# Holding back the last 16 sorted tiles for late tokens, with the last stage's lead-in beside them and the zero fills on SyncE's queue

## What is computed

```python
h = _L0_tok_ref(x, ...)                        # (64, 128, 256): rows of two tables
h = h + _L0_attn_ref(_layernorm(h), W_qkv, ...)     # linear attention, 16 heads
h = h + _L0_ffn_ref(_layernorm(h), sim_matrix, gates, q_proj, k_proj, v_proj, o_proj)

# in _L0_ffn_ref, E = 16 experts, HD = 128
rw = _gating(hidden_states, sim_matrix, gates)      # (b, t, E), two entries a token here
q = jnp.einsum('btc,ech,bte->bth', hidden_states, q_proj, rw)     # k and v alike
scores = jnp.where(causal[None], jnp.einsum('bqh,bkh->bqk', q, k) * scale, -jnp.inf)
ao = jnp.einsum('bqk,bkh->bqh', jax.nn.softmax(scores, axis=-1), v)
out = jnp.einsum('bth,ehc,bte->btc', ao, o_proj, rw)
```

## Time and profile before

| | |
|---|---|
| median of three executions | 995.45 us (992.7, 995.45, 995.6) |
| the profiled execution's own time | 992.72 us |
| its span, first to last instruction | 990.9 us |
| mean granted TensorE clock | 0.987 of full |
| busy in the span | PE 925.8, DVE 838.2, POOL 668.9, ACT 600.0 us |
| moved by DMA | 137.54 MB, mean 139 GB/s |

### The profile page before, as it was taken

How to read it: one execution, slowest core, us unless ns; L and a number is a source line. 1 busy time by engine, 2 the same in 40 slices (tenths; PEclk the granted TensorE clock), 3 DMA queues, 4 the chain that set the end, 5 groups by cost and what they waited for, 6 DMA issues and landing times.

```text
span 990.9 us, 20545 instructions
## 1 busy us (share of the span) xinstructions
PE 925.8 (93%) x5231; PEld 798.1 (81%) x5231; DVE 838.2 (85%) x2910; ACT 600.0 (61%) x1633; POOL 668.9 (68%) x881
## 2 busy tenths in 40 slices
PE   4999999999899989989999599999999999999998
PEld 4777788887777889979899578888888888888876
DVE  3789999999999987556665369999999999999998
ACT  4566676676667554435444266666666766666664
POOL 5447777777777655795000268888888888888885
PEclk9999999999999999989999889999999999999999
DMA  2113444444343349878898423333333333333231
GB/s 66 49 60 123 127 130 155 144 149 130 113 128 115 99 159 333 281 251 274 279 294 266 156 84 104 107 107 107 107 98 103 100 100 107 107 107 103 90 102 38
DMA packets 104762, 137.54 MB, mean 139 GB/s; under 512 B 13762, under 2 KB 91586, under 8 KB 104644
## 3 DMA queue, kind: packets, MB, share of 16 engines
q1 hardware_dynamic: 86196, 82.93, 26.6%
q0 software_dynamic: 18176, 52.45, 17.4%
q10 hardware_dynamic: 272, 0.79, 0.2%
HBM read 70.06 MB, written 66.06 MB: 137 GB/s over the span
## 4 chain that ended last, share of the span: by engine, by line
PE 60%; DVE 26%; issue 6%; POOL 3%; DMA 2%; ACT 2%; SPq 1%; POOLq 0%; DVEq 0%; ACTq 0%
PE bank L1655 16%; PE bank L1656 16%; PE bank L1657 16%; PE bank L1662 6%; DVE phi L1302 4%; DVE attn L1245 2%; DVE kvm L1321 2%; DVE stats L1258 2%; PE bank L1681 2%; DVE stats L1079 2%; DVE zden L1243 1%; PE bank L1899 1%; PE bank L1905 1%; POOL sorted_x L786 1%; DVE moments L1260 1%
## 5 line engine op out<-in xcount | busy, mean ns | idle before, releaser
L1655 PE MATMUL bank<-wo_hi,split_lo 128*128 128x512 f32 x512 | 214.6, 419 | 1.5 <-DVE split_lo L1623 0.8
L1656 PE MATMUL bank<-wo_lo,split_hi 128*128 128x512 f32 x512 | 203.3, 397 | 0.0
L1657 PE MATMUL bank<-wo_hi,split_hi 128*128 128x512 f32 x512 | 203.3, 397 | 0.0
L860 POOL DMA_INDIRECT row_y<-sorted_y,pair_now x128 | 130.7, 1021 | 31.2 <-issue 22.3
L1009 ACT ACTIVATE h<-bank,rwo 128x256 f32<-128x256 f32 x256 | 106.8, 471 | 26.5 <-PE bank L1657 13.9
L1657 PEld LDWEIGHTS bank<-wo_hi,split_hi 128*128 128x128 f32 x512 | 96.8, 189 | 23.1
L1655 PEld LDWEIGHTS bank<-wo_hi,split_lo 128*128 128x128 f32 x512 | 96.9, 189 | 21.5 <-DVE x L1592 1.6
L1592 DVE SCALAR_TENSOR_TENSOR x<-bank,rwo,x 128x256 f32<-128x256 f32 x256 | 111.1, 475 | 1.2 <-PE bank L1657 1.2
L1656 PEld LDWEIGHTS bank<-wo_lo,split_hi 128*128 128x128 f32 x512 | 97.5, 190 | 17.5
L1592 DVE SCALAR_TENSOR_TENSOR qk_e<-bank,rwo,qk_e 128x256 f32<-128x256 f32 x256 | 110.9, 474 | 0.2 <-PE bank L1657 0.2
L1655 PE MATMUL bank<-wq_hi,split_lo 128*128 x288 | 110.6, 384 | 0.0
(11 more groups left out here) (242 smaller groups left out, 2529.4 us busy)
## 6 DMA issues: line engine op xcount, KB each, us to landing
sorted_y<-w_attn SPq DMA_DIRECT2D x40, 384.0 KB, 3.4
sorted_y<-row_y SPq DMA_DIRECT2D x24, 384.0 KB, 3.6
h_rows<-h SPq DMA_DIRECT2D x64, 128.0 KB, 1.7
row_x<-h_rows SPq DMA_DIRECT2D x64, 128.0 KB, 3.5
out_h<-row_x SPq DMA_DIRECT2D x64, 128.0 KB, 2.1
h<-sorted_x SPq DMA_DIRECT2D x48, 128.0 KB, 3.3
phi<-sorted_x SPq DMA_DIRECT2D x24, 128.0 KB, 3.5
qk_neg<-sorted_x SPq DMA_DIRECT2D x24, 128.0 KB
```

What stands on the lines that cost most here:

```text
L860: pool.indirect_dma_start(out=row_y[:, 2 * tile.p + n, :], out_offset=None, in_=sorted_y, in_offset=offsets(pair_now[tile.q][:, n:n + 1])) ...
L1655: pe.matmul(ps, left[1][c], right[0][c], start=(c == 0), stop=False)
L1656: pe.matmul(ps, left[0][c], right[1][c], start=False, stop=False)
L1657: last = pe.matmul(ps, left[0][c], right[0][c], start=False, stop=(c == n - 1))
```

## The change

- Of the sorted tiles, the last LATE = 16 slots (128 to 143) now hold only tiles that the first KEPT = 4 sequences can't need. In four sequences an expert gets at most 4 x 128 rows, that is its first four tiles; the late slots are filled from what an expert has beyond those. `final_table` has 26 operations instead of 17 for this, over 33 segments (16 middle, one of spare tiles, 16 late), and POOL's rounds for `pair_at` become 47.
- POOL gathers the rows of tiles 0 to 3 as soon as the stores up to slot 127 have landed (`middle_stored`), and the lead-in of steps -4 to -1 is spread over steps 136 to 144 of stage 2 on ACT, DVE and PE (`lead_in`). From slot 120 on the products go to three other buffer pairs (`raw`, the gate's `top_both`, `x2_more`), since `row_y` and `w_attn` are wanted by the lead-in. `run3` begins at step 0. In the dense way the lead-in follows as before.
- The 16 zero fills are plain DMAs from SP, one in each of steps 20 to 35, with row numbers from a register; the wait for tables, fills and scatters stands in step 38 instead of 36. N_X goes from 12 to 11.
- Four constants more are set by POOL at the start, in five memsets.

```diff
-    N_X = 12
+    N_X = 11
+    KEPT, LATE = 4, 16
+    LATE_FROM = PAIR_TILES - LATE
+    LATE_Y = LATE_FROM - 8
+    SEGS = 2 * E + 1
...
         x_buf = [h4[:, q, :] for q in range(4)] + [b[:, c * C:(c + 1) * C] for b in (phi, qk_neg, qk_e) for c in range(2)]
-        x_buf += [x1[:, :], attn[:, :]]
+        x_buf += [x1[:, :]]
...
+            elif tile.c < LATE_Y:
+                pair, m = y_pair, (tile.c - EARLY) % 8
             else:
-                pair, m = y_pair, (tile.c - EARLY) % 8
+                pair, m = y_pair_late, (tile.c - LATE_Y) % EARLY_Y
...
+            m = tile.c - LATE_Y
+            if m < EARLY_Y:
+                eng.wait_ge(weights_lo, 4 * E)
+            else:
+                eng.wait_ge(y_stored_late[m % EARLY_Y // 2], 16 * (m // EARLY_Y))
...
+        def middle_stored(eng):
+
+            early_stored(eng)
+            for sem_ in y_stored:
+                eng.wait_ge(sem_, 16 * ((LATE_Y - EARLY) // 8))
+            for n in range(3):
+                stores = len([c for c in range(LATE_Y, LATE_FROM, 2) if (c - LATE_Y) % EARLY_Y // 2 == n])
+                eng.wait_ge(y_stored_late[n], 16 * stores)
...
         def run3(eng, step):
-            for c in range(-4, B + 1):
+            for c in range(B + 1):
...
-                if c + N_X == EARLY:
+                if c == 20:
+                    sp.wait_ge(fill_ready, 1)
+                if 20 <= c < 20 + E:
+                    half, n = divmod(c - 20, E // 2)
+                    if n == 0:
+                        fills.update(enumerate(fill_rows(sp, half)))
+                    sp.dma_start(sorted_x[bass.ds(fills[n], P), :], zeros[:, :]).then_inc(regions_filled, 16)
+                if c + N_X < EARLY:
+                    load_pair(Tile(c + N_X))
+                if c == 38:
                     sp.wait_ge(tables_ready, 1)
                     sp.wait_ge(regions_filled, 16 * E)
                     sp.wait_ge(dummies_zeroed, 16 * E)
                     for t in range(B - N_X2, B):
                         scatter_done(sp, t)
-                load_pair(Tile(c + N_X))
+                    load_pair(Tile(EARLY))
+                if c >= 38:
+                    load_pair(Tile(c + N_X))
                 if c >= 2 and c % 2 == 0:
                     store_pair(Tile(c - 2))
...
                 run2(sp, step2)
-                early_stored(sp)
-                for q in range(4):
-                    sp.wait_ge(y_stored[q], 16 * ((PAIR_TILES - EARLY) // 8))
+                sp.wait_ge(routed, 1)
+                step3(Tile(-1))
+                for n in range(3):
+                    sp.wait_ge(y_stored_late[n], 16 * ((PAIR_TILES - LATE_Y) // EARLY_Y))
                 sp.sem_inc(y_ready, 1)
...
+            branch(sp, sorted_way, dense_way)
             run3(sp, step3)
...
+            pool.memset(start[:, E:E + 1], float(E * REGION)).then_inc(consts_ready, 1)
+            pool.memset(weight[:, 0, 0:E - 1], 1.0).then_inc(consts_ready, 1)
+            pool.memset(weight[:, 0, E - 1:E + 1], 0.0).then_inc(consts_base, 1)
+            pool.memset(weight[:, 0, E + 1:SEGS - 1], 1.0).then_inc(consts_ready, 1)
...
-            pool.wait_ge(fill_ready, 1)
-            for e in range(E):
-                pool.indirect_dma_start(out=sorted_x, out_offset=offsets(fill_at[:, e:e + 1]), in_=zeros[:, :],
-                                        in_offset=None).then_inc(regions_filled, 16)
...
-                for n in range(2 * E - 1):
-                    e, later = (n + 1) // 2, n % 2 == 0
+                limits = (region_start[:, :], later_start, late_start)
+                for n in range(3 * E - 1):
+                    e, part = (n + 1) // 3, (n + 1) % 3
...
+                middle_stored(pool)
+                for c in range(-4, 0):
+                    step3(Tile(c))
...
+            def lead_in(k):
+
+                if k == 136:
+                    first_rows(Tile(0))
+                if k == 138:
+                    heads_copied(Tile(0))
+                    first_rows(Tile(1))
+                if k == 140:
+                    exponentials(Tile(0))
+                if k == 142:
+                    probs_copied(Tile(0))
+                    heads_copied(Tile(1))
+                if k == 143:
+                    first_rows(Tile(2))
+                if k == 144:
+                    ao_high(Tile(0))
+
             def step3(i):
...
 
+            def first_free_rows():
+                quad_done(dve, "rank_product", last_group)
+                link(dve.tensor_tensor(next_row[:, :], ps_count, region_start[:, :], ALU.add))
+                dve.tensor_copy(fill_i[:, :], next_row[0:1, :]).then_inc(fill_ready, 1)
...
+            N_FINAL_OPS = 26
...
+                if k == 19:
+                    first_free_rows()
...
+            def lead_in(k):
+
+                if k == 136:
+                    second_rows(Tile(0))
+                if k == 138:
+                    second_rows(Tile(1))
+                if k == 139:
+                    scores_limited(Tile(0))
+                if k == 141:
+                    probs_inverse(Tile(0))
+                if k == 143:
+                    scores_limited(Tile(1))
+                if k == 144:
+                    second_rows(Tile(2))
+                    ao_low(Tile(0))
+
...
+                if k == 34:
+                    pe.wait_ge(table_v, 24)
...
+            def lead_in(k):
+
+                if k == 137:
+                    heads_turn(Tile(0))
+                if k == 139:
+                    scores_product(Tile(0))
+                if k == 141:
+                    probs_turn(Tile(0))
+                    heads_turn(Tile(1))
+                if k == 143:
+                    ao_product(Tile(0))
+                    scores_product(Tile(1))
```

More of the change, by code:

```diff
@@ L504, in run3, with fill_rows @@
         def run3(eng, step):
-            for c in range(-4, B + 1):
+            for c in range(B + 1):
                 step(Tile(c))
+        def fill_rows(eng, half):
+            n = E // 2
+            return nc.values_load_multi_w_load_instructions(
+                fill_i[0:1, half * n:(half + 1) * n], engines=(eng.engine,), min_val=0, max_val=E * REGION - P,
+                skip_runtime_bounds_check_because="a region's start and at most B * T counted rows")[1]
         def every_tile(eng, step):
@@ L1013, in step3 @@
                 if tile.inside(B):
[L1014 to L1016 removed]
+                    exponentials(tile)
                 if i.inside(B):
```

357 lines of the change are left out of this document (210 added, 147 removed).

## The result

The changed kernel takes 982.14 us (median of 4 runs, 981.2 to 983.13), the kernel before, run beside it, 995.32: a ratio of 0.9874, 95% interval 0.9853 to 0.9894. Predicted were 974 and at most 982. The direction was right and the size was not: 13 us came instead of 21. The two profiled executions have spans of 990.9 and 979.5 us, so the trace accounts for 11.4 us; the one of before was the quickest of its four (992.7).

The account below looks back on a forecast made before the run. PE bounds the kernel, so only its holes can pay: seam 14.5, gate 6.7, start -0.2, in all 21.0 us off the median 995.45, giving 974; range 968 to 982.

Parts of the forecast that it names:

- The lead-in moves and is in time: Seam of stages 2 and 3: lead-in adds 0.77 us before T (last expert product's end), no stall; gain 13.0 us.
- rival 1: End of stage 2: gathers come late and stop ACT, hence PE, for 3 to 5 us; 976 to 980, chance 0.13.
- The jump, 0.4: Seam: jumping over the other branch's code, now on the path, costs 0.4 us; bounds 0 and 2.
- The clock, 1.95: Seam: with a hole of 1.9 us full clock stays, so the first nine wo products give back 1.95 us.
- The gate, 6.7: Wait at tile 48: its 7.7 us go, less 1.0 for the store queue, worth 6.7 us.
- the 1.0 for the store queue: Steps 20 to 35: fills beside loads and stores on SP cost PE 1.0 us; bounds 0 and 3.5.
- the last at about 411: Stage 2, SP's queue: the last zero fill goes out at about 411 us, two to five us before the wait.
- Rival 3: Gate at tile 48: fills land late behind a full DMA queue, most of 6.7 us is lost; 980, chance 0.09.
- Stage 3's step, 6.38: Last stage: the step stays at 6.38 us, PE's own work; the prediction is wrong if it moves.
- Rival 4: Last stage: the loop settles into PE waiting for DVE every step, eating the 21 us; 999 or more, chance 0.02.

Follow-up runs that it names:

- number 3: The changed kernel with the whole last stage written into both ways, so the jump stands behind it: 977.68 us, ratio 0.9849.
- number 8: The changed kernel with each fill issued behind its step's load and store, and fill rows read by fours: 979.33 us, ratio 0.9853.
- number 9: The changed kernel with the 16 zero fills shared, 8 on GpSimd and 8 on the sync queue, one every second step: 982.12 us, ratio 0.9878.
- numbers 4: The kernel before without the dense way, the sorted way standing alone on every engine: 997.11 us, ratio 1.0039.
- number 1: The changed kernel run again with no edit: 981.59 us, ratio 0.9878.
- numbers 17 and 18: The kernel before without GpSimd's one-column addition, first with the dense way (990.96 us, ratio 0.9973), then without it (991.39 us, ratio 0.9976).

## Why the prediction was off, step by step

**The lead-in moves and is in time: right.** In tiles 86 to 143 it cost 1.2 us instead of 0.8, PE didn't wait for rows or heads in its last steps, and rival 1 didn't come (PE waits for nothing between 540 us and T). The low half was ready at T+1.97 (forecast T+2.3 for PE's start; number 3 has it at T+2.10).

**The jump, 0.4: the step that failed first.** I let 1.7 us of it be covered, since PE "reaches its jump at T+0.6", and took 0.4 of an unknown price. In the trace it cost 564.91 - 560.35 - 2.10 = 2.5 us in line. By the covered part the price would be some 4 us from the jump's turn to the first product. The instruction packets in the earlier trace rows had been read only as a time at which something was fetched, not as how long the engine lacked it; in after the second of two comes at 563.65, 2.7 us after the jump's turn. The Trainium skill ("Runtime: NRT & Kernel Launch", Instruction fetch mechanics) has the rule that a taken branch out of the loaded window stalls. The 13 profiles of the table agree with it (packets move in the gap only where the jump is), and put 2.4 to 3.0 us on it for PE where nothing else fills the time.

**The clock, 1.95: failed with it.** The hole was 4.1 us and not 1.9, so the clock fell: the nine products took 3.7 (gain 0.3). Where the hole is 2 us (number 3), it stays. The two terms are one: 3.9 us for 2.5 of stall.

**The gate, 6.7: the larger miss.** That SP would hardly wait for fills was right (0.7 us left). The step that failed is the 1.0 for the store queue, and with it "the last at about 411": it was 417.2. Of the 6.7 came 1.6. I argued from "2 loads, 2 fills and 1 store in 2.54 us, as it has later with weight loads", and from where PE lost 0.95 us. That compares what is issued, and never adds up what the queue needs: 2.7 us without a single read of rows, 3.4 with them. The register reads weren't in the sum at all, but number 8 had the fills' reads at half the price and lost as much, so they aren't what decides. Rival 3 had the size (most of 6.7 lost) with another mechanism, fills that land late because the DMA is full, which number 9 excludes. The gate's 7.7 was also a high reading of 6.0 to 8.0.

**Stage 3's step, 6.38: right for after, and luck.** Rival 4 named the danger (the loop settling into another order) and priced it 0.02. In the changed kernel it costs 5 steps as before. In numbers 4 and 9 the stage went over at step 47 and at step 41, and took back 5 and 8 us. I had looked at DVE's 370 of 385 us and not at GpSimd's, 322, which shows busy time but not that its step has 0.25 us of room.

**Tiles 74 to 86: not foreseen and not explained.** 2.8 us went there in after, 1.9 in number 1; the other kernels of the change lose 2.1 to 3.7, those of before 1.6 to 2.6. PE waits for DVE there, as before, while the output weights load. GpSimd's address rounds now run beside it, but they do so in the kernels that lose little as well. No run was made that takes the rounds away, so this stays open.

## What to carry to other kernels

A jump is free while its engine has something to wait for. A change that removes the wait brings the jump onto the path, here 2.5 us and 1.4 to 2 of clock; write what follows into both arms, or put the jump where an engine waits anyway. Before moving DMAs to another queue, add up what that queue needs in one step, register reads included, and compare it with the step: half the fills on each of two queues won 4.8 us where all on one won nothing. And when an edit shows its gain in the trace but not in the time, look for a later stage that has two paces.

## What the runs showed of the hardware that I hadn't expected

- A taken jump over the dense way's code makes PE's next product 2.4 to 3.0 us later, in 8 kernels out of 8, against the 5 without one there. Where the engine waits over 8 us anyway it costs nothing (numbers 17 and 18).
- Reading 8 values into registers on the sync engine took 1.2 and 1.5 us in after, as much as two to three DMA issues, and 0.5 to 1.3 in the other kernels that do it; reading 4 took 0.3 to 1.3. The price varies more with the moment than with the count.
- DVE and GpSimd operations on SBUF hold each other up: 0.74 becomes 1.17, 0.41 becomes 0.89, and a one-column addition 0.43 instead of 0.19. That makes two stable paces of one loop, 6.38 and 6.75 us.
- In each of the twenty profiles the time from one indirect gather to the next, 1.3 us, is 1.0 to 1.5 us longer at one place: behind the 113th that GpSimd issues for the last stage, whatever the time (890 to 917 us). With the one-column addition the stage ran at 6.75 after it almost to its end, without it at 6.38. What it is, no run shows.
